# Early-fusion embed kernel: text tiles among the image steps, rows normalised on POOL, stacked table rows, odd image columns on ACT's queue

## What is computed

```
out  = einsum('bnd,ed->bne', patchify(images), W_proj) + b_proj + pos_emb
text = weights[_positions(tokens)]                    # 34 rows of the table are in reach
h = concatenate([out, text], axis=1)
h = h + attn(layernorm(h))      # three projections (dt, x, g) of layernorm(h), a convolution, a state-space sum
h = h + ffn(layernorm(h))       # four experts, two per row
```

## Time and profile before

| | |
|---|---|
| median of 3 runs | 499.2 us (497.4 to 500.18) |
| span of the profiled execution, first to last instruction | 495.2 us |
| busy: PE, DVE, ACT, POOL | 442.5, 330.5, 296.4, 152.2 us |
| mean granted TensorE clock | 0.967 of full |
| the stage that the change touches | 0 to about 68.6 us |
| image halves split by DVE | 13.85 to 34.0 us |
| image tiles on PE | 34.16 to 63.2 us |

### The profile page before, as it was taken

The page is one execution under the profiler, slowest core; times in us unless marked ns, Lnnn a source line. Parts: engine busy times, 40 slices in busy tenths (PEclk is TensorE's granted clock), DMA queues, the critical chain, the costliest instruction groups (busy, mean ns, idle before and its releaser), DMA issues.

```text
span 495.2 us, 9980 instructions
## 1 busy us (share of the span) xinstructions
PE 442.5 (89%) x3149; PEld 363.4 (73%) x3149; DVE 330.5 (67%) x980; ACT 296.4 (60%) x667; POOL 152.2 (31%) x255
## 2 busy tenths in 40 slices
PE   8989989799899999999999798999999999999400
PEld 5769967667778878887777577888878888888300
DVE  6885567678999434335786777866674666666584
ACT  2854359177975465316554354887786777877341
POOL 2000000000000000001243887874778644543322
PEclk9999999799999999999999999999999999999955
DMA  7981089900019942972511222232322333252262
GB/s 178 187 228 56 33 253 322 292 0 2 1 35 259 217 114 58 228 228 81 180 54 52 89 94 77 86 97 66 107 98 76 107 107 110 74 155 69 78 213 82
DMA packets 58734, 59.94 MB, mean 121 GB/s; under 512 B 25368, under 2 KB 51260, under 8 KB 57404
## 3 DMA queue, kind: packets, MB, share of 16 engines
q1 hardware_dynamic: 54236, 48.68, 36.4%
q0 software_dynamic: 3552, 9.74, 5.3%
q10 hardware_dynamic: 896, 0.89, 0.6%
HBM read 34.50 MB, written 24.80 MB: 120 GB/s over the span
## 4 chain that ended last, share of the span: by engine, by line
PE 66%; DVE 12%; issue 7%; ACT 7%; POOL 4%; DMA 2%; SPq 1%; DVEq 0%; POOLq 0%; ACTq 0%
PE bank L1040 14%; PE bank L881 9%; PE bank L433 8%; PE bank L435 8%; PE bank L434 8%; PE bank L955 3%; PE bank L1030 3%; PE bank L901 3%; POOL sorted_x L671 2%; PE bank L1012 2%; ACT U L470 1%; DVE spj L1400 1%; DMA got<-expert_y 1%; PE bank L848 1%; PE bank L947 1%
## 5 line engine op out<-in xcount | busy, mean ns | idle before, releaser
L1040 PE MATMUL bank<-w,hr 128*128 x320 | 76.0, 380 | 1.5 <-DVE ysb L1661 1.5
L1040 PEld LDWEIGHTS bank<-w,hr 128*128 128x128 f32 x320 | 60.1, 190 | 11.7 <-issue 2.7
L644 POOL MEMSET ones<- 2x128 f32 x1 | 0.2, 194 | 212.3 <-PE bank L916 212.3
L1234 ACT ACTIVATE hr<-bank,gsel 128x128 f32<-128x128 f32 x160 | 59.9, 460 | 0.2 <-PE bank L1030 0.2
L719 POOL DMA_INDIRECT expert_y<-ysb,toid x40 | 42.8, 1071 | 51.3 <-DVE ysb L1661 34.7
L881 PE MATMUL bank<-Tb,U 68*32 68x68 f32 x1024 | 45.9, 358 | 0.3 <-issue 0.3
L881 PEld LDWEIGHTS bank<-Tb,U 68*32 68x32 f32 x1024 | 40.6, 139 | 3.6 <-issue 3.1
L1646 DVE BATCH_NORM_STATS2 bsth<-bank 128x6 f32<-128x512 f32 x40 | 27.7, 693 | 20.5 <-PE bank L435 20.2
L671 POOL DMA_INDIRECT sorted_x<-x2s,slot x34 | 33.8, 994 | 15.3 <-issue 9.2
L1226 ACT ACTIVATE hn<-bank,nmrh,rsh 128x512 f32<-128x512 f32 x40 | 31.1, 777 | 10.0 <-DVE nmrh L1655 8.1
L433 PE MATMUL bank<-w_hi,bT_hi 128*128 x80 | 35.0, 438 | 0.1
(11 more groups left out here) (297 smaller groups left out, 1153.3 us busy)
## 6 DMA issues: line engine op xcount, KB each, us to landing
Tb<-ssm_kernels SPq DMA_DIRECT2D x16, 680.0 KB, 7.5
sorted_x<-zpad SPq DMA_DIRECT2D x6, 1419.0 KB, 13.6
xg<-sorted_x SPq DMA_DIRECT2D x40, 129.0 KB, 2.1
got<-expert_y SPq DMA_DIRECT2D x17, 256.0 KB, 3.6
XI<-in_x_dram SPq DMA_DIRECT2D x12, 288.0 KB, 5.6
h0r<-h_spill SPq DMA_DIRECT2D x17, 128.0 KB, 2.1
out_dram<-acc SPq DMA_DIRECT2D x17, 128.0 KB
w1raw<-in_L_ffn_w_dram SPq DMA_DIRECT2D x4, 512.0 KB, 15.9
```

The source lines that it names most:

```text
L1040: mm = pe.matmul(bank[6][:, 0:D], hr[:, i % 3, c, :], w2[:, bass.ds(expert[i], 1), c, :].rearrange("p o n -> p (o n)"), start=(c == 0), st ...
L1234: last = act.activation(hr[:, i % 3, c, :], bank[3 + i % 2][:, c * P:(c + 1) * P], ACT.Relu, scale=gsel[:, i, 0, c:c + 1], bias=gsel[:, i, ...
```

## The change

- Order: six text tiles (`EARLY`) with four `img` jobs each, then rounds: text 15 with image 0, text 16 with image 1, then one image tile each. A tile's a4 comes two rounds behind its a1 (three before).
- The normalisation into `xs` goes from DVE to POOL, behind two new casts that make `sel` there. DVE keeps the reciprocal.
- The hi and lo rows of the text table stand stacked in one tile (`tabl_hl`: hi at partition 0, lo at 64; `OH` has 98 partitions), so a text tile is one matmul; the same for `posb_hl`, so an image tile has one matmul fewer.
- DVE makes `posb_hl` behind the first four `img` jobs (step `rows`), not at the start.
- SP issues the even image columns, ACT the odd ones: three ahead of its Exp and three behind its Ln. The stacked tables take two more DMAs on SP and two more on ACT.
- `warm` ahead of `img` jobs is gone.
- `BLOCK_ORDER` is [0, 3, 4, 1, 2] instead of [3, 4, 0, 1, 2].
- Tiles are spilled one by one; semaphores `h0_stored` and `got_in` become `row_moved`.

```diff
+        EARLY = 6
+        TEXT, IMAGE = list(range(NTI, NT)), list(range(NTI))
+        ROUNDS = [TEXT[EARLY + r:EARLY + r + 1] + [i] for r, i in enumerate(IMAGE)]
+        TILE_ORDER = TEXT[:EARLY] + [t for ts in ROUNDS for t in ts]
-        BLOCK_ORDER = [3, 4, 0, 1, 2]
+        BLOCK_ORDER = [0, 3, 4, 1, 2]
...
-        for k in range(NT + 3):
-            A_STEPS += [(f"a{s + 1}", TILE_ORDER[k - s]) for s in (3, 2, 1, 0) if 0 <= k - s < NT]
-            count = 3 if k < NH0 else 1
-            A_STEPS += [("ring", q) for q in ahead[:count]]
...
+        each = len(IMAGES) // EARLY
+        for r in range(EARLY):
+            A_STEPS += take(1) + [("a4", t) for t in TEXT[r - 2:r - 1] if r >= 2] + [("a1", TEXT[r])] + take(1)
+            A_STEPS += [("a3", t) for t in TEXT[r - 1:r]] + take(each - 2)
+            A_STEPS += [("a2", TEXT[r])] + ([("rows",)] if r == 0 else [])
+        ROUNDS = [[t] for t in TEXT[EARLY - 2:EARLY]] + ROUNDS
+        for r in range(2, NTI + 4):
+            done, held, new = (ROUNDS[n] if n < NTI + 2 else [] for n in (r - 2, r - 1, r))
+            A_STEPS += [("a2", t) for t in held if t < NTI or t >= TEXT[EARLY]] + take(1) + [("a3", t) for t in held]
+            A_STEPS += [("a1", t) for t in new[:-1]] + [("a4", t) for t in done] + [("a1", t) for t in new[-1:]]
+            if r >= NTI + 2:
+                A_STEPS.append(("dt", r - NTI - 2))
...
-            sp.dma_start(tabl[:], ins["L0_txt_weights"][0:LT + 2, :]).then_inc(sem("table_in"), 16)
+            for r0, r1 in ((0, LT + 2), (LT + 2, SECOND), (SECOND, TH)):
+                sp.dma_start(tabl[r0:r1], ins["L0_txt_weights"][0:r1 - r0, :]).then_inc(sem("vecs_in"), 16)
             for g in range(2):
-                for wp in range(HP):
+                for wp in range(0, HP, 2):
...
+            for m, i in enumerate(TILE_ORDER):
+                pool.wait_ge(sem("rs0"), m + 1)
+                pool.wait_ge(sem("h0_copied"), m + 1)
+                if m >= 2:
+                    pool.wait_ge(sem("xT_ps"), m - 1)
+                pool.tensor_scalar(xs[:, m % 2, :], h0s[:, m % NH0, :], mv0[:, i, 0:1], rs0[:, i:i + 1], ALU.subtract,
+                                   ALU.mult).then_inc(sem("x"), 1)
...
-                    elif kind == "img":
-                        warm(ps, 1)
...
-                        pe.matmul(ps, at_i, tabl_hi[:], start=True, stop=False)
-                        mm = pe.matmul(ps, at_i, tabl_lo[:], start=False, stop=True)
+                        mm = pe.matmul(ps, OH[:, (i - NTI) * P:(i - NTI + 1) * P], tabl_hl[:], start=True, stop=True)
...
-                        pe.matmul(ps, at_i, posb_hi[:], start=False, stop=False)
-                        mm = pe.matmul(ps, at_i, posb_lo[:], start=False, stop=True)
+                        mm = pe.matmul(ps, at_i, posb_hl[:], start=False, stop=True)
...
+            def odd_columns(g):
+
+                for wp in range(1, HP, 2):
+                    act.dma_start(XI[:, g, wp].rearrange("p (y k) -> p y k", k=PWC),
+                                  img[g][:, :, wp * PWC:(wp + 1) * PWC]).then_inc(sem(f"img_in{g}{wp // 2}"), 16)
...
             act.preload_act_table_set("natural_log_exp_and_others")
+            odd_columns(0)
             act.wait_ge(sem("a_capped"), 1)
             act.activation(atmp[:], atmp[:], ACT.Exp).then_inc(sem("a_exp"), 1)
             act.wait_ge(sem("a_exp"), 1)
             act.wait_ge(sem("consts"), 6)
             act.activation(atmp[:], atmp[:], ACT.Ln, bias=onec[:]).then_inc(sem("a_exp"), 1)
+            odd_columns(1)
...
-                    link(dve.reciprocal(rs0[:, i:i + 1], sd0[:, i:i + 1]))
-                    if m >= 2:
-                        dve.wait_ge(sem("xT_ps"), m - 1)
-                    dve.tensor_scalar(xs[:, m % 2, :], h0s[:, m % NH0, :], mv0[:, i, 0:1], rs0[:, i:i + 1], ALU.subtract,
-                                      ALU.mult).then_inc(sem("x"), 1)
+                    dve.reciprocal(rs0[:, i:i + 1], sd0[:, i:i + 1]).then_inc(sem("rs0"), 1)
```

More of the change, by code:

```diff
@@ L295, in build_kernel, with take @@
         ahead = list(range(len(PREP), len(A_RING)))
-        for k in range(NT + 3):
-            A_STEPS += [(f"a{s + 1}", TILE_ORDER[k - s]) for s in (3, 2, 1, 0) if 0 <= k - s < NT]
-            count = 3 if k < NH0 else 1
-            A_STEPS += [("ring", q) for q in ahead[:count]]
-            ahead = ahead[count:]
-            if k in (NT, NT + 1):
-                A_STEPS.append(("dt", k - NT))
+        def take(count):
+            steps = [("ring", q) for q in ahead[:count]]
+            del ahead[:count]
+            return steps
+        each = len(IMAGES) // EARLY
[10 more added lines that the diff above has]
+                A_STEPS.append(("dt", r - NTI - 2))
         assert not ahead
@@ L426, in h0_out @@
         def h0_out(eng):
-            for n in range(len(H0_OUT)):
-                eng.wait_ge(sem(f"h0_stored{n}"), 32 if n == len(H0_OUT) - 1 else 16)
+            for n in range(NH0):
+                eng.wait_ge(sem(f"row_moved{n}"), 16 * spilled(n))
         def split3(pe, out_ap, a_hi, a_lo, b_hi, b_lo, start, stop):
@@ L610, in _ @@
                       allow_small_or_imprecise_dtypes=True).then_inc(sem("consts"), 1)
+            pool.wait_ge(sem("consts"), 6)
+            pool.wait_ge(sem("zpad"), 2)
+            pool.tensor_copy(sel[0:SECOND], ident[0:SECOND, 0:LI].rearrange("p (t o) -> p t o", o=1).broadcast_to(
+                [SECOND, LI, B])).then_inc(sem("consts"), 1)
+            pool.wait_ge(sem("consts"), 7)
+            pool.tensor_copy(sel[SECOND:], ident[SECOND:IH, SECOND:IH].rearrange("p (t o) -> p t o", o=1).broadcast_to(
+                [LI, LI, B])).then_inc(sem("consts"), 1)
+            pool.wait_ge(sem("consts"), 8)
+            for m, i in enumerate(TILE_ORDER):
[5 more added lines that the diff above has]
+                                   ALU.mult).then_inc(sem("x"), 1)
             for p in range(2):
@@ L766, in _ @@
                         k = rest[0]
-                        mm = pe.matmul(ps[0:LT + 2, :], ones_b[:, 0:LT + 2],
+                        mm = pe.matmul(ps[0:TH, :], ones_b[:],
                                        posD[:].rearrange("p j b -> p (j b)")[:, k * 512:(k + 1) * 512],
@@ L1078, in _ @@
                     continue
-                if step[0] == "dt":
+                if step[0] in ("dt", "rows"):
                     continue
@@ L1343, in _ @@
                     continue
+                if step[0] == "rows":
+                    dve.wait_ge(sem("pos_in"), 64)
+                    link(dve.tensor_tensor(posb[:], posb[:], bpb[:], ALU.add))
+                    dve.tensor_copy(posb_hl[0:SECOND], posb[0:SECOND]).then_inc(sem("posb"), 1)
+                    signal(dve.tensor_copy(posb_hl[SECOND:], posb[SECOND:]), "posb", 9)
+                    dve.tensor_tensor(posb_hl[SECOND:], posb[SECOND:], posb_hl[SECOND:].bitcast(F32), ALU.subtract).then_inc(
+                        sem("posb"), 1)
+                    continue
                 if step[0] == "dt":
```

73 lines of the change are left out of this document (29 added, 44 removed).

## The result

The changed kernel takes 507.5 us (median of 4 runs, 506.7 to 508.2) against 498.3 for the kernel before: a ratio of 1.0188 (95% interval 1.016 to 1.0216), 1.9% slower. The forecast was 497.8 with a range to 503.5. The profiled execution has a span of 506.3 beside 495.2, 11.1 us more. Places inside the first stage can agree much better: three kernels of the second table that share this stage reach the third dt projection at 61.8, 62.1 and 62.3. The argument goes by such places, of one execution each, and by the medians, and says where the two differ.

A forecast was written before the change was run, and what follows sets the result against it. DVE was taken to bound the kernel's first stage up to 34 us, then PE. Image phase +1.9, image tiles -2.0, tail -0.8, block order -0.5 sum to -1.4: 499.2 becomes 497.8 us, range 490.5 to 503.5.

The forecast's parts named there:

- the sixteen other `xs` cost nothing: POOL is idle in this stage: First stage: `xs` on POOL, apart from the last tile's, adds 0 us while DVE has work elsewhere.
- 24 halves ... together 16.2: Image phase: DVE's work from the first half, summed by instruction, takes 16.2 us, so the halves end at 35.95.
- the tail: End of last image tile to third dt projection: 4.6 us instead of 5.4, so -0.8.
- POOL's price: One `xs` on POOL, in the tail: 0.79 us taken, between bounds of 0.41 and 0.79, plus a 0.1 hop.
- ACT's hold: Start of first stage: six column issues hold ACT until 17.1; first half reaches DVE at 19.75 instead of 13.85; +1.9.
- 4.0 us of slack: Image phase: without the wait for ACT, DVE's halves would have ended 4.0 us or more early.
- Image tiles: PE's 29.0 us of image tiles gets shorter, mainly by nine fewer `sel` matmuls; -2.0, PE staying the bound.
- Block order: PE's wait for DVE behind the first four dt projections shrinks from 3.65 to about 3.4 us; -0.5 taken.
- if it falls as before, 0: Block order: no gain if the clock falls to 1.2 GHz as before; 0.9 us back if it holds.
- The first: Rival: ACT isn't held by its column issues, halves end at 30.05, -7.3, 491.9 us; chance 0.24.
- The second's condition: Rival: PE stays at 1.2 GHz through the halves and into the image tiles; +3.9, 503.1 us; chance 0.20.

The follow-up runs named there:

- three kernels of the second table: Changed kernel with columns on SP and `xs` on DVE: 492.0 us; also with the old block order: 490.9; that with filling among the dt projections: 488.7.

## Why the prediction was wrong, by its own steps

- **The step that failed: "the sixteen other `xs` cost nothing: POOL is idle in this stage".** An idle engine was read as a free one. It was priced by its busy time alone; that its result is waited for by PE, ahead of the halves that DVE needs next, was not followed round. That DVE's work bounds the halves ("24 halves ... together 16.2") rests on DVE never waiting. It took 21.3 us from the first half to the end of the last in the changed kernel, 15.4 where a4 was moved: the sum over DVE's instructions was right to within 0.9, and the assumption under it wrong. In its place the runs showed a ring of 3.83 us a round where DVE's work was 2.66. `xs` back on DVE gave 8.6 us, of which 0.85 is the tail, the one `xs` that was priced; with the columns on SP, moving a4 alone gave 7.0 by the medians and 4.8 at `adt`.
- **POOL's price** was a mis-sized term: 0.79 taken between 0.41 and 0.79, measured 1.22. The 789 ns of the earlier trace rows are for two tensor inputs, but the nearest row of another operation is no bound. The Trainium skill (GPSIMD Engine Reference, Engine selection) has one-input work on POOL at about line rate. The trace differs for this form, one tensor input with two per-partition scalars: 1.22 us on POOL, 0.41 on DVE. The measurement decides. The tail came out at 4.72 for 4.6, as other parts of it were shorter.
- **ACT's hold** was right in its mechanism and 1.3 us short: ACT free at 18.38 for 17.1, first half at 20.89 for 19.75. Issues of 2.9 us in the second group agree with the 3.0 predicted; the first three took 0.68, 1.45 and 3.35, where 0.75, 0.75 and 2.9 had been reckoned. The Trainium skill (DMA: Bandwidth & Descriptors, Issuing engines are not separate DMA queues) says that DMAs from several engines run on the same 16 DMA engines. On that the trace agrees, 197 GB/s beside 194. The DMA share of 1.01, read as full, was no sign of it: it was 1.44 with two queues at the same GB/s. The mis-sized term is what the hold costs: +1.9, with 4.0 us of slack set against it. Undoing it alone gave 6.6, and that slack didn't exist with POOL in the loop.
- **Image tiles:** -2.0 predicted. Without POOL they take 25.7 us at full clock, 3.3 under the 29.0 before; in the changed kernel PE's waits for POOL cost 1.8 and the cold clock 1.8 more, which with 25.7 leaves 0.2 of the 29.5 open. The term had the right sign and was 1.3 short. Some 0.9 of that is in the stacked `sel` matmul, which takes 0.12 us to the next start (46.90 to 47.02 in the changed kernel) where each of the two before took 0.22. Two costs ate the gain, of which one stood nowhere and one in a rival.
- **Block order:** -0.5 predicted with 0 as its worst; +1.4 measured. The step was "if it falls as before, 0": it took the half-clock stretch to be as long as before, and it got longer.
- **The rivals.** The first didn't happen: ACT was held. The second's condition did, and its price in part: a round is 3.83 us with PE cold and 3.50 warm, by about the 0.3 that it named, and the image tiles lost 1.8 where it had 3.0. But that is the price inside the loop that POOL had closed, which no rival had, and with DVE full the cold halves took 17.8 us and the warm ones 18.1. Its 503.1 lay nearer to the result than the forecast, and still 4.4 under it.
- **What was right** is hidden in the sum: the new order of tiles, the stacked rows and `sel` on POOL, without the odd columns on ACT and without `xs` on POOL, are worth 1.3% with either block order, and 1.7% with the block order of before and the wait filled. They were not run one by one.

## To carry to other kernels

Before work goes to an idle engine, write down who needs the result, what stands behind that consumer in its order, and whether the producer waits for any of it: if the chain closes, its length is the new round. Here it was enough to move the consumer behind the work that the producer waits for (5 to 7 us). A DMA issue belongs on an engine with nothing due: six column issues held ACT for 14.1 us. A clock that fell cost nothing where DVE was full, and cost where PE or a chain through PE set the pace; and filling that was free at full speed became the pace at half, with the odd columns on ACT alone.

## What the runs showed of the hardware that was not expected

- A busy PE can stay at half clock for long: with odd columns on ACT alone, it was busy 4.00 of each 4 us from 20 to 36 us, nearly half of it with filling matmuls, and the granted clock stayed at 0.50 (1.2 GHz). With columns on SP and a4 later there is no filling, and the clock, at 0.57 from 20 to 25 us, was at 1.0 from 25 to 30.
- A wait of 1.54 us, with PE's busy time in the 5 us around it down from 4.37 to 3.46, came ahead of a fall to half (the kernel before with `xs` on POOL); 1.43 us ahead of the first image matmul did not, with 3.52 us of PE's work from 30 to 35 us.
- POOL's subtract-and-multiply with two per-partition scalars on 128x256 numbers takes 1.22 us, three times DVE's 0.41, and nearly the same at each of 17 places (1218 to 1255 ns).
